# A decoder layer on one core: gamma and beta in 16-byte pieces, x transposed by every fourth column, x's second half one weight chunk later

## The reference, cut to what matters

```
x = layernorm(x + attn(x))     # the stage that this change touches
x = layernorm(x + xattn(x))    # fp8 round trip of x and ctx, then a product
x = layernorm(x + ffn(x))      # SwiGLU and 8 of 1024 experts per token

def attn(X, W_in, b_in, W_out, b_out, gamma, beta):       # X: 4 x 512 x 512
    Xn = layernorm(X) * gamma + beta
    Q, K, V = split(Xn @ W_in + b_in, 3)                  # W_in: 512 x 1536
    K, V = rotary(K), rotary(V)
    A = sum over tokens of cos_sim(K) * cos_sim(V)
    return ((0.5 * A + 0.5) * Q) @ W_out + b_out + X
```

## Time and profile before

| | us |
|---|---|
| median of 3 executions | 790.91 (790.62 to 791.0) |
| the profiled execution's own time | 791.2 |
| its span in the profile | 789.4 |
| busy: PE, PEld | 775.0 (98%), 637.9 (81%) |
| busy: DVE, POOL, ACT | 664.5 (84%), 360.5 (46%), 322.0 (41%) |

### The profile page before, as it was taken

One profiled execution on the slowest core, in us unless ns is written; L12 is line 12 of the kernel. 1 busy time (PEld: TensorE's weight loads), 2 busy tenths in 40 slices (PEclk: granted clock), 3 DMA queues, 4 the chain that ended last, 5 costly groups with the idle time before them and its releaser, 6 DMA issues.

```text
span 789.4 us, 10701 instructions
## 1 busy us (share of the span) xinstructions
PE 775.0 (98%) x3586; PEld 637.9 (81%) x3590; DVE 664.5 (84%) x1348; ACT 322.0 (41%) x704; POOL 360.5 (46%) x313
## 2 busy tenths in 40 slices
PE   8999999999899999999999999999999999999997
PEld 7888888887678778888888888888888888888885
DVE  6888679998898871476779998999999999899876
ACT  5454336456574422223443433343333343344324
POOL 1241222232122411014476676775776677676324
PEclk9999999999999999999999999999999999999999
DMA  8656504624455629001122221331233323242014
GB/s 318 252 128 167 94 0 101 174 76 75 76 142 117 149 90 295 1 1 32 50 77 81 83 88 41 118 104 47 86 113 110 92 79 113 63 128 62 16 54 159
DMA packets 51334, 79.92 MB, mean 101 GB/s; under 512 B 17519, under 2 KB 26479, under 8 KB 50768
## 3 DMA queue, kind: packets, MB, share of 16 engines
q0 software_dynamic: 24240, 31.52, 19.1%
q1 hardware_dynamic: 25456, 47.72, 17.4%
q10 hardware_dynamic: 1584, 0.01, 0.1%
HBM read 110.64 MB, written 12.58 MB: 156 GB/s over the span
## 4 chain that ended last, share of the span: by engine, by line
PE 65%; DVE 3%; issue 2%; POOL 2%; ACT 1%; POOLq 0%; ACTq 0%; DVEq 0%
PE gu L1883 14%; PE gu L1884 14%; PE gu L1885 14%; PE ob L1957 6%; PE ob L1956 6%; PE ob L1961 6%; PE ob L1910 1%; POOL h_lo L1311 1%; DVE scratch L1575 1%; DVE x_lo L1622 1%; DVE scratch L1577 0%; PE gu L2055 0%; DVE xall L1616 0%; PE ob L1977 0%; POOL xall L153 0%
## 5 line engine op out<-in xcount | busy, mean ns | idle before, releaser
L1883 PE MATMUL gu<-x_hi,w_hi 128*128 128x512 f32 x516 | 201.4, 390 | 0.0
L1885 PE MATMUL gu<-x_hi,w_lo 128*128 128x512 f32 x516 | 200.8, 389 | 0.0
L1884 PE MATMUL gu<-x_lo,w_hi 128*128 128x512 f32 x516 | 200.7, 389 | 0.0
L1311 POOL TENSOR_TENSOR h_lo<-mid,h_hi 128x512 fp32r<-128x512 f32 x62 | 86.8, 1417 | 175.4 <-ACT h_hi L1461 175.4
L1885 PEld LDWEIGHTS gu<-x_hi,w_lo 128*128 128x128 f32 x516 | 96.8, 188 | 20.2
L1883 PEld LDWEIGHTS gu<-x_hi,w_hi 128*128 128x128 f32 x516 | 96.9, 188 | 20.0
L1884 PEld LDWEIGHTS gu<-x_lo,w_hi 128*128 128x128 f32 x516 | 96.9, 188 | 19.9
L1471 ACT ACTIVATE gates<-dots 128x1 f32<-128x1 f32 x144 | 29.2, 203 | 175.2 <-DVE dots L1724 175.2
L1633 DVE TENSOR_TENSOR mid<-gu,mid 128x512 f32<-128x512 f32 x64 | 44.0, 687 | 64.1 <-PE gu L1885 54.2
L1956 PE MATMUL ob<-w_hi,h_hi 128*128 128x512 f32 x224 | 87.1, 389 | 0.0
L1957 PE MATMUL ob<-w_lo,h_hi 128*128 128x512 f32 x224 | 87.1, 389 | 0.0
(11 more groups left out here) (254 smaller groups left out, 1438.1 us busy)
## 6 DMA issues: line engine op xcount, KB each, us to landing
stage<-in_ctx SPq DMA_DIRECT2D x7, 1024.0 KB, 5.8
total<-prod POOLq DMA_DIRECT2D x11, 384.0 KB, 4.1
xall<-half_bo POOLq DMA_DIRECT2D x4, 1024.0 KB, 9.2
xhat<-in_L_ffn_gate_w SPq DMA_DIRECT2D x8, 512.0 KB, 3.5
xhat<-in_L_ffn_up_w SPq DMA_DIRECT2D x8, 512.0 KB, 3.8
xall<-in_mask_Bx1xS_ff POOLq DMA_DIRECT2D x4, 1024.0 KB, 11.0
xhat<-in_L_ffn_down_w SPq DMA_DIRECT2D x8, 512.0 KB, 3.6
x_dram<-xall SPq DMA_DIRECT2D x4, 1024.0 KB, 7.8
```

Source lines behind the costliest of these rows:

```text
L1311: nc.gpsimd.tensor_tensor(lo[:, c], mid[c][:], hi[:, c].bitcast(F32), ALU.subtract).then_inc(hlo_done, 1)
L1883: nc.tensor.matmul(dst, lhs[0], rhs[0], start=start, stop=False)
L1884: nc.tensor.matmul(dst, lhs[0], rhs[1], start=False, stop=False)
L1885: return nc.tensor.matmul(dst, lhs[1], rhs[0], start=False, stop=stop)
```

## The change

The features are dealt out differently: chunk c now holds features 4p+c. Gamma and beta then are 16 contiguous bytes per partition, W_in's chunk c is every fourth row, and the transposes read every fourth column of `xhat`, for all four batches. The identity moves from SP's queue to ACT's, behind gamma and beta; the query bias, still in 4-byte pieces, moves from ACT's to SP's, behind x of batch 1. The first half of x is loaded as two transfers of one tile each, with a semaphore each, and the statistics of tile 0 start when it is in.

For chunk 0 of part 0, ACT writes `xn_hi` straight from the bank, and DVE computes `xs` itself, after `low_w(0)`. ACT's later `scaled_x` waits for the `xs` before it. On DVE the statistics of part 1 move behind `low(0, 1)`, and its `normalise(1)` behind `low(0, 2)`; on PE the transposes of part 1 move from before chunk 2 to before chunk 3. The zero products go from 16 to 12.

```diff
-IDLE_PRODUCTS = 16
+IDLE_PRODUCTS = 12
...
-    w_in_v = w_in.rearrange("(c p) n -> c p n", p=P)
+    w_in_v = w_in.rearrange("(p c) n -> c p n", c=KC)
...
-                sp.dma_start(xall[:, 0:2 * D], x_tiles[0][:, 0]).then_inc(x_half, 16)
-                sp.dma_start(ident[:], consts[:, C_ID:C_ID + P]).then_inc(ident_in, 16)
+                for i in range(2):
+                    sp.dma_start(xall[:, i * D:(i + 1) * D], x_tiles[0][:, 0, i * D:(i + 1) * D]).then_inc(x_tile[i], 16)
...
                 load_x(1)
+                sp.dma_start(b_q[:], b_in[0:D].rearrange("(c p) -> p c", p=P), allow_slow_non_contiguous=True).then_inc(bq_in, 16)
...
-                for dst, src, count in ((gam, gamma, gb_in), (bet, beta, gb_in), (b_q, b_in[0:D], bq_in)):
-                    act.dma_start(dst[:], src.rearrange("(c p) -> p c", p=P), allow_slow_non_contiguous=True).then_inc(count, 16)
+                for dst, src in ((gam, gamma), (bet, beta)):
+                    act.dma_start(dst[:], src.rearrange("(p c) -> p c", c=KC)).then_inc(gb_in, 16)
+                act.dma_start(ident[:], consts[:, C_ID:C_ID + P]).then_inc(ident_in, 16)
...
+                    act.wait_ge(xs_done, j)
...
-                    high(0, c)
+                    if c == 0:
+                        act.wait_ge(xt_mm, 1)
+                        nc.scalar.activation(xn_hi[:, 0, part_cols(0)], x_bank(0, 0)[:, part_cols(0)], ACT.Identity, scale=gam[:, 0:1], bias=bet[:, 0:1]).then_inc(hi_done, 1)
+                    else:
+                        high(0, c)
...
-                dve.wait_ge(x_half, 16)
-                x_stats(0, (0, 1))
+                for i in range(2):
+                    dve.wait_ge(x_tile[i], 16)
+                    x_stats(0, (i,))
                 x_variance(0)
                 normalise(0)
                 low_w(0)
+                dve.wait_ge(gb_in, 32)
+                dve.wait_ge(hi_done, 1)
+                nc.vector.tensor_scalar(xs[:, 0, part_cols(0)], x_bank(0, 0)[:, part_cols(0)], gam[:, 0:1], bet[:, 0:1], ALU.mult, ALU.add).then_inc(xs_done, 1)
+                dve.wait_ge(xs_done, 1)
                 low(0, 0)
+                low_w(1)
+                low(0, 1)
                 dve.wait_ge(x_in[0], 16)
                 x_stats(0, (2, 3))
                 x_variance(1)
-                low_w(1)
-                low(0, 1)
+                low_w(2)
+                low(0, 2)
                 normalise(1)
-                for c in range(2, KC):
-                    low_w(c)
-                    low(0, c)
+                low_w(3)
+                low(0, 3)
...
-                        last = nc.tensor.transpose(x_bank(p, c)[:, i * P:(i + 1) * P], xhat[:, i, c * P:(c + 1) * P], ident[:])
+                        last = nc.tensor.transpose(x_bank(p, c)[:, i * P:(i + 1) * P], xhat[:, i].rearrange("p (q c) -> p c q", c=KC)[:, c], ident[:])
...
-                    if k == 2:
+                    if k == KC - 1:
                         for c in range(KC):
                             transposes(1, c)
```

More of the change, by code:

```diff
@@ L200, in decoder_layer @@
             x_in = [sem(f"x_in{b}") for b in range(B)]
-            x_half = sem("x_half")
+            x_tile = [sem("x_tile0"), sem("x_tile1")]
             w_raw = [sem(f"w_raw{c}") for c in range(KC)]
@@ L266, in _ @@
                 sp.dma_start(trig[:].rearrange("p a b -> p (a b)"), consts[:, C_TRIG:C_TRIG + TB * 3 * P]).then_inc(trig_in, 16)
-                sp.dma_start(qT[:], w_in.rearrange("(c p) n -> p c n", p=P)[:, :, 0:D]).then_inc(wq_raw, 16)
+                sp.dma_start(qT[:], w_in.rearrange("(p c) n -> p c n", c=KC)[:, :, 0:D]).then_inc(wq_raw, 16)
                 load_x(1)
+                sp.dma_start(b_q[:], b_in[0:D].rearrange("(c p) -> p c", p=P), allow_slow_non_contiguous=True).then_inc(bq_in, 16)
                 sp.dma_start(half_bo[:], b_out.partition_broadcast(P)).then_inc(hb_in, 16)
@@ L1004, in _ @@
                 for k in range(KC):
-                    if k == 2:
+                    if k == KC - 1:
                         for c in range(KC):
                             transposes(1, c)
-                    if k == KC - 1:
                         for i in range(2):
```

## The result

The changed kernel takes 793.01 us (median of 10; 792.51 to 793.66), the kernel before 790.96 (median of 10; 790.62 to 791.53). The ratio is 1.0025, 95% interval 1.0017 to 1.0033: 2.0 us slower. The profiled execution took 793.49 us with a span of 791.7; it is one of the slower of its ten, 0.5 above their median.

The account below looks back on a forecast made before the run. PE bounds the kernel, through tile 2's start. Chunk 1's landing 1.85 us earlier is returned nearly whole by later transposes and bias: tile 2 at 22.9 against 23.02, 0.1 earlier, 790.8 us. Range 790.0 to 796.3; the forecast's own 790.3 to 791.7.

Parts of the forecast that it names:

- The path and its exchange rate: First batch's tile 2 on PE: any microsecond earlier or later is passed on whole; PE work added after 23 us too.
- What the opening gives back: PE before tile 2: later part 1 transposes and the bias behind them start tile 2 at L + 14.0, PE idling 1.5 us.
- L: Landing of chunk 1's weights, where ACT waited: 10.75 before the change, forecast 8.9, bounds 10.75 and 8.35.
- the chain behind part 1 does not bind: Rival: ACT and DVE run part 1 faster, PE goes dense from chunk 0; 1.2 us gained, 789.7; chance 0.08.
- What the opening gains: Transfers before chunk 1: fewer gamma and beta packets gain 1.45 us, b_q's leaving 0.4; L falls to 8.9.
- The hole between x and the weights: Slow DMA from 3.5 to 5.5, 2.0 us, laid to gamma's and beta's packets with the identity; forecast to shrink to 0.55.
- the split of x and the identity's move to the other queue bring nothing more: Opening: chunk 0's products end at 10.6, hidden behind chunk 1's wait until 10.9, so these edits gain nothing.
- Reading every fourth column: Transposes of all batches, 48 in batches 1 to 3: taken as zero; upper bound 0.11 us each, 5.3 over 48.
- The rival's doubling: Rival of slow strided transposes in batches 1 to 3: up to 0.11 us more each, 796.2 us; chance 0.28.
- Four zero products fewer cost nothing: Start of PE: 24 passes end at about 6.6 instead of 7.6, while transposes wait for `xhat` until about 7.2.
- The clock rival: Opening on PE: standing still after twelve zero products keeps or drops the clock at 1.2 GHz; 3 us, 794; chance 0.04.
- costs them the same 0.4: SP's queue: b_q delays half_bo, mix and iota8 by 0.4 us; iota8 lands near 21.6 to 22.5, no longer last.

Follow-up runs that it names:

- e1: Changed kernel with the identity's transfer back on SP's queue, behind x's two tiles: 792.57 us.
- e2: Kernel before with only the new order: PE's part 1 transposes before chunk 3, DVE's part 1 statistics and normalisation one chunk later: 792.65 us, ratio 1.0018.
- e17: Changed kernel with sixteen zero products again: 793.41 us.
- e13: Changed kernel with x's first half in one transfer and the identity on SP: 792.43 us.
- e10: Changed kernel with DVE's bias addition of tile 0 moved between low(1, 1) and low(1, 2): 792.85 us.
- e6: Kernel before with the new dealing of features, gamma and beta in 16-byte pieces, and b_q on SP behind x of batch 1: 791.25 us.
- e7: As e6, but W_in's rows and the transposed columns dealt as in the kernel before: 790.48 us.
- e12: Changed kernel with x whole, identity on SP, mix and iota8 ahead of half_bo, b_q last, tile 0's bias addition between low(1, 1) and low(1, 2): 791.61 us.
- e19: e6 with the identity's transfer third on ACT's queue, behind gamma and beta: 791.75 us.
- e14: Changed kernel with x's first half in one transfer, identity still on ACT's queue: 793.03 us.
- e18: e6 with the first half of x in two transfers and tile 0's statistics begun early: 791.36 us.
- e3: Changed kernel with the part 1 order of the kernel before on PE and DVE: 792.38 us.
- e16: e6 with mix and iota8 ahead of half_bo, b_q last, and DVE's part 1 statistics ahead of low_w(1) and low(0, 0): 790.76 us, ratio 0.9994.
- e4: Kernel before with only features dealt as 4p+c in W_in's rows and the transposed columns: 791.89 us, ratio 1.0013.

## Why the prediction was wrong

- *The path and its exchange rate*: right. A later tile 2 was paid in full: 1.88 of the 2.3 us between the two profiled executions, the transposes behind it being the rest.
- *What the opening gives back*: right, and closest of all. "L + 14.0" was measured as L + 14.00, 14.01 and 14.01 in e1, e2 and e17, L + 14.15 in the changed kernel and L + 14.33 in e13, with the releaser and the idle time as described (1.27 for 1.5). The rival "the chain behind part 1 does not bind" is refuted by e2; in e10 another wait replaced it.
- *What the opening gains*: this is the step that failed. "L goes from 10.75 to 10.75 - 1.45 - 0.4 = 8.9" was measured as 10.75, and as 10.92, 10.82 and 9.91 in the three variants with the same transfers: a gain between nothing and 0.8 us in place of 1.85. Two errors are in it. The term was too large: with the small pieces gone and nothing else moved in front of chunk 1, L was 9.6 in e6 and e7, which is 1.15 and perhaps a little more, and less in e12 and e13 (10.37, 9.98). The hole between x and the weights stayed 1.25 us long with a quarter of the pieces in the changed kernel, where 0.55 was forecast, so a good part of it was never theirs. And "the split of x and the identity's move to the other queue bring nothing more" was held for a reason to price them at zero. The identity landed at 8.35 instead of 5.67, 6.7 us after its issue; with it back on SP's queue L was 10.24 and the time 0.4 us less (e1). I had named the outcome: with L = 10.75 "it would give 792.7". The other 0.3 is within what the columns and the low clock cost.
- *Reading every fourth column*: taken as zero, measured 0.01 us a transpose, 0.5 us in all by the spacings and 0.6 to 0.8 us by the medians. The rival's doubling (0.11) is refuted. The weight load did take 71 ns more (211 for 140), and most of it found room beside the matmuls, so the reason for the choice of zero was half right. The Trainium skill's note (SBUF — State Buffer, on SBUF cachelines) asks for two hits on a line for full bandwidth; the trace agrees that one hit costs something, half of a load's time again, but a tenth of the 0.109 from one transpose to the next.
- *Four zero products fewer cost nothing*: nearly right. The clock rival's place was right, its price too high: PE stood still from 6.8 to 8.4, and from 10.0 to 13.3 the products were 0.43 apart, but chunk 0 had slack, and 0.15 to 0.3 is what reached tile 2 (L + 14.15 and L + 14.33 against L + 14.0).
- *b_q on SP's queue "costs them the same 0.4"*: wrong in kind. The issue behind b_q's took 4.42 us, iota8 was issued 3.8 us later, and it landed at 23.3 (forecast 21.6 to 22.5), and at 24.2 in e10.
- Two readings in the prediction are a little off: 791.0 + 5.3 is 796.3 and not 796.2, and the slices behind the hole are 263 and then mostly 377 and more, with 313 to 329 among them. Nothing rests on either.

By the medians: order +1.6 (e2), columns +0.6 to 0.8, identity on ACT +0.4 to 0.6 (e1, e19, e14 against e13), split +0.1 (e18), low clock up to 0.3, pieces and b_q -0.6; the sum of 2.1 to 2.8 stands against 2.0 measured. Only the order is clear of the noise by a wide margin. The other terms are each known to some tenths and can overlap, so that the sum comes near is no proof of its parts.

Left open: why L is 10.75 to 10.9 in three of the four profiles that have both the split and the identity on ACT (changed, e3, e10), and 9.6 to 10.4 in all with the small pieces gone and one of the two at most. By the slices of DMA traffic the bytes up to chunk 1 had been moved by 9.5 in the changed kernel, 0.5 earlier than before, and ACT still started at 10.75; in e12, with neither, they had been moved another 0.5 earlier, and L was 10.37. What holds the landing back is not shown.

## What to carry to other kernels

A gain at the head of a chain counts only after the moves that were made to reap it are priced in the same chain: here 1.85 us of hoped-for landing was spent in advance on transposes placed 3.1 us later. Look for the instruction that stands in order behind the moved one on another engine (here a bias addition behind four `xn_lo`), since it frees the bank that the main engine needs next. And price a change of queue for each transfer by what was measured on that queue, not by its bytes: the 64 KB of the identity took 5.8 to 6.8 us from issue to landing on ACT's queue, and 2.9 to 4.6 on SP's. Last, take L from more than one execution: the same transfers gave values up to 1.0 us apart.

## What the runs showed of the hardware

A transpose's weight operand read in steps of 16 bytes takes 211 ns to load instead of 140, for 128 fp32 columns (e6 against e7), and the transposes start 0.12 us apart instead of 0.109.

With twelve zero products the granted clock fell to 0.50 for about 3.4 us in four of seven profiles: the changed kernel, e3, e10 and e13. In these PE had stood still for 1.58, 1.42, 2.00 and 1.61 us between the zero products and the transposes, and the clock fell after it was at work again (at 10.0 in the changed kernel). In the other three, e1, e12 and e14, the pause was 0.31, 0.96 and 1.34 us. No profile with sixteen had a low clock in the opening, but none had a pause above 0.75 us either, so the runs do not separate the number of products from the pause.

The landing of chunk 0 with 288 small packets on ACT's queue instead of 1584 (x whole, identity on SP) was 6.93, 6.93, 7.05, 7.27 and 7.76 in e6, e7, e16, e13 and e12; with 1584 it was 7.67, 7.66 and 8.11 in the kernel before, e2 and e4. So it comes sooner in most executions, by up to 0.7 us, and not in every one.

The issue that follows the 512 four-byte pieces of b_q on SP's queue took 4.42 us in the changed kernel; in the kernel before, the issue in that place took 1.20.
